# Spectral attention as one unrolled program: transform, attention and taps of three batches side by side, the gate applied in the frequency domain, the next router's logits inside

## The chip, the cores and the metric

One core of one Trainium2 chip. The metric is device time in microseconds (us) of one execution of the whole program, which holds nine blocks of a small hybrid network; the change rewrites one of them and takes in a small one behind it.

## The reference, cut to what matters

The rows are 8,192 tokens (8 batches of 1,024) of 256 channels. Two blocks of the chain are touched: the spectral attention with its residual, and the router logits that the next mixture of experts needs. In each batch, 16 chunks of 64 tokens are transformed:

```python
Xh = jnp.fft.rfft(chunks, axis=2)                  # 33 bins of each chunk and channel
X_low, X_high = Xh[:, :, :4, :], Xh[:, :, 4:, :]
A_low = complex(attention(X_low.real), attention(X_low.imag))   # 16 heads, 4 kv heads, 64 tokens
H_r, H_i = causal_conv(X_high.real), causal_conv(X_high.imag)   # 7 taps, gelu, 256x256 product
g = sigmoid(chunks.mean(axis=2) @ gate_w.T)[:, :, None, :]
A_high = complex(H_r * g, H_i * g) + X_high
Y_hat = concatenate([alpha * A_low + (1 - alpha) * X_low, A_high])
x = x + irfft(Y_hat, n=64)                         # on the layer-normed x; then logits = x @ Wg.T
```

All products are float32.

## The kernel before

`R.X` keeps all rows on the core, as 64 tiles of 128 tokens by 256 channels (8 tiles a batch). Each engine has its own queue, written out by hand; semaphores order them. A `Stage` ends with a barrier of all engines, so nothing of one stage lies beside another. `skewed` writes a loop whose phases run a fixed number of steps behind each other.

`spectral_attention` (L818) is four stages, each over all eight batches, and `raw_logits` (L283) is a fifth:

- **Weights** (`turned_copies`, L782): seven loads, 52 transposes by TensorE, 13 copies by ScalarE (L815).
- **Transform** (L850): VectorE normalizes a tile (L904), TensorE multiplies it by the Fourier matrix (L878), VectorE copies it into the spectrum `XF` (L909). At the end the gates of all chunks are made (L886 to L920) and stored to DRAM.
- **Attention** (L925): an unrolled loop over batches. TensorE makes queries (L955), keys (L961), values (L968), scores (L979, zero-padded queries, 128 rows deep), transposes of the shares (L989), the weighing (L997), the output product (L1004). VectorE makes the softmax (L1081 to L1090) with its exponential on ScalarE (L1042). ScalarE copies the rest.
- **Convolution and inverse** (L1097): sixteen steps of four tiles. VectorE runs 28 tap instructions a step over four accumulators (L1229, L1233), ScalarE the gelu (L1175), TensorE the channel product (L1137), ScalarE its copy (L1184), TensorE the inverse (L1148), the low pass of the normalized tile (L1149) and the inverse of the low bins (L1150). VectorE multiplies by the gate in the time domain (L1213), adds the low term (L1214), normalizes again (L1205) and takes the statistics (L1219). GpSimd adds twice (L1269, L1271).
- **Logits** (`raw_logits`): per tile two transposes (L314), one copy (L335), two products with eight columns (L322). Beside them the rows go out to `sum_dram`.

## Time and profile before

| | |
|---|---|
| median of three runs | 4252.68 us (4248.62 to 4254.37) |
| profiled execution | 4250.82 us, its span 4248.8 us |
| five stages above | from 752.7 to 1374.8 us of the span, 622.1 us |

The profile comes from one execution. PE is the TensorE matmul, PEld its weight load, DVE is VectorE, ACT ScalarE, POOL GpSimd. Two records of a float32 matmul belong together (two passes of two), but a transpose is one record. PEclk is the granted TensorE clock as a share of full speed.

### The profile page before, as it was taken

How to read it: one execution, taken by the hardware profiler on the slowest of the kernel's cores; microseconds unless marked ns; L12 is line 12 of the kernel's file. 1: busy time of each engine (PE TensorE's matmuls, PEld its weight loads, DVE VectorE, ACT ScalarE, POOL GpSimd, SP SyncE). 2: the span in 40 equal slices, each digit the busy share in tenths (PEclk: the TensorE clock that was granted, in tenths of full speed). 3: DMA queues.
4: the chain of work that ended last, by engine and by line, in shares of the span. 5: the costliest groups of instructions: out<-in, count | busy, mean ns of one | idle time of the engine just before them, and what ended most of it. 6: DMA issues, size and time to landing. Idle time of an engine off the chain costs nothing. (4 is left out here: it accounts for less than half of the span.)

```text
span 4248.8 us, 118480 instructions
## 1 busy us (share of the span) xinstructions
PE 3765.7 (89%) x44654; PEld 3235.7 (76%) x44654; DVE 2500.6 (59%) x6817; ACT 2036.2 (48%) x6280; POOL 1392.2 (33%) x1780
## 2 busy tenths in 40 slices
PE   8957998696668499969999999999998799999998
PEld 7857998584437499958888888888885477777775
DVE  5565555536992655544444444444446588888885
ACT  3344554132221555523443443434434488888884
POOL 2225664001331466523333333333333222222214
PEclk9978999797895699989999999999999899999999
DMA  3033444100002444330000000000000000000002
GB/s 109 31 121 97 93 93 110 39 1 26 28 29 94 144 93 93 61 109 3 3 3 3 3 3 3 3 3 3 3 3 9 15 2 2 2 2 2 2 2 88
DMA packets 138456, 162.53 MB, mean 38 GB/s; under 512 B 11984, under 2 KB 128624, under 8 KB 137968
## 3 DMA queue, kind: packets, MB, share of 16 engines
q1 hardware_dynamic: 113392, 122.17, 9.1%
q0 software_dynamic: 24576, 33.57, 4.6%
q8 instruction: 340, 5.57, 0.5%
q14 instruction: 148, 1.21, 0.1%
HBM read 96.85 MB, written 58.85 MB: 37 GB/s over the span
## 5 line engine op out<-in xcount | busy, mean ns | idle before, releaser
L1955 ACT ACTIVATE wa_S<-wa_S,wa_top 128x256 f32<-128x256 f32 x1024 | 511.7, 506 | 139.2 <-DVE wa_top L2019 138.4
L1614 DVE TENSOR_TENSOR so_AB<-so_rows,so_masks 128x1024 f32<-128x1024 f32 x256 | 313.5, 1224 | 243.3 <-PE so_rows L1358 226.1
L2019 DVE CUSTOM_DVE_ANT_0 wa_S<-wa_bank,wa_band 128x256 f32<-128x256 f32 x1024 | 366.9, 419 | 8.4 <-issue 8.3
L1673 POOL TENSOR_TENSOR so_state<-so_compact,so_head 128x384 f32<-128x384 f32 x224 | 185.3, 827 | 335.5 <-PE so_bankC L1425 248.0
L1881 PE MATMUL wa_bank<-ident,wa_S 128*128 128x128 f32 x2048 | 274.4, 275 | 22.2 <-ACT wa_probT L1962 22.2
L1603 DVE SCALAR_TENSOR_TENSOR so_compact<-so_compact,so_bankX 128x96 f32<-128x96 f32 x192 | 48.8, 254 | 414.3 <-PE so_bankX L1461 414.3
L1881 PEld LDWEIGHTS wa_bank<-ident,wa_S 128*128 128x128 f32 x2048 | 230.6, 141 | 67.2 <-ACT wa_S L1955 31.2
L1386 PE MATMUL so_bankJ<-so_xnT,so_w 128*128 128x128 f32 x2048 | 251.5, 276 | 1.2 <-ACT so_QT L1523 0.7
L1386 PEld LDWEIGHTS so_bankJ<-so_xnT,so_w 128*128 128x128 f32 x2048 | 240.4, 193 | 1.9 <-ACT so_QT L1523 1.0
L1549 ACT COPY so_OT<-so_bankC 128x128 f32<-128x128 f32 x256 | 68.1, 266 | 307.7 <-PE so_bankC L1425 307.7
L1668 POOL TENSOR_TENSOR so_Ug<-so_U,so_decay_t 128x128 f32<-128x128 f32 x224 | 102.2, 456 | 325.4 <-ACT so_U L1536 325.4
L1955 ACT ACTIVATION_READ_ACCUMULATOR wa_S<-wa_S,wa_top 128x1 f32 x1024 | 199.3, 195 | 0.0
L713 ACT ACTIVATE m2e_hT<-m_bank,m2e_bias 128x256 fp32r<-128x256 f32 x256 | 126.6, 494 | 150.9 <-PE m_bank L665 145.1
L713 ACT ACTIVATE m4e_hT<-m_bank,m4e_bias 128x256 fp32r<-128x256 f32 x256 | 126.3, 493 | 148.5 <-PE m_bank L665 142.3
L1269 POOL TENSOR_TENSOR spc_high<-spc_high,spc_low 128x256 f32<-128x256 f32 x64 | 49.6, 775 | 447.8 <-DVE spc_low L1214 447.8
L2027 DVE COPY wa_probT<-wa_bank 128x512 f32<-128x512 f32 x256 | 166.9, 687 | 48.3 <-PE wa_bank L1881 47.0
L665 PE MATMUL m_bank<-m2e_exT,m_w_parts 128*128 128x256 f32 x1536 | 190.0, 283 | 0.3 <-ACT m2e_h L713 0.3
L665 PE MATMUL m_bank<-m4e_exT,m_w_parts 128*128 128x256 f32 x1536 | 189.9, 283 | 0.1
L679 PE MATMUL m_bank<-m_w_parts,m4e_hT 128*128 128x256 f32 x1536 | 189.5, 282 | 0.6 <-DVE m4e_pre L760 0.6
L679 PE MATMUL m_bank<-m_w_parts,m2e_hT 128*128 128x256 f32 x1536 | 189.5, 282 | 0.6 <-DVE m2e_pre L760 0.6
L679 PEld LDWEIGHTS m_bank<-m_w_parts,m2e_hT 128*128 128x128 f32 x1536 | 186.3, 188 | 0.8 <-issue 0.8
L679 PEld LDWEIGHTS m_bank<-m_w_parts,m4e_hT 128*128 128x128 f32 x1536 | 186.2, 188 | 0.8 <-issue 0.8
(411 smaller groups left out, 10556.6 us busy)
## 6 DMA issues: line engine op xcount, KB each, us to landing
m_w_raw<-in_L_ffn_W_dram SPq DMA_DIRECT2D x64, 512.0 KB, 3.9
sum_dram<-X SPq DMA_DIRECT2D x16, 1024.0 KB, 4.9
X<-sum_dram SPq DMA_DIRECT2D x16, 1024.0 KB, 7.1
X<-in_L_attn_a_x_dram SPq DMA_DIRECT2D x8, 1024.0 KB, 11.5
xn_dram<-m2r_xn SPq DMA_DIRECT2D x16, 512.0 KB, 3.1
spc_gx<-gate_dram SPq DMA_DIRECT2D x128, 64.0 KB, 2.5
xn_dram<-m4r_xn SPq DMA_DIRECT2D x16, 512.0 KB, 3.1
out_dram<-X SPq DMA_DIRECT2D x8, 1024.0 KB, 4.4
```

The costliest lines, as they stand in the source:

```text
L665: last = nc.tensor.matmul(bank[:, 0:2 * P], w_parts[:, par, a, c, f * P:(f + 1) * P], exT[:, s % 2, b, c], start=(n == 0), stop=(n == len( ...
L679: last = nc.tensor.matmul(by[u][:, 0:HID], hT[:, s % 2, a, f, u * P:(u + 1) * P], w_parts[:, par, b, 2 + f // QF, f % QF * HID:(f % QF + 1 ...
L713: last = nc.scalar.activation(to, bh[f % 4][:, 0:2 * P], ACT.Gelu_apprx_tanh, bias=bias[:, par, f:f + 1])
L1386: last = nc.tensor.matmul(bJ[:, k * P:(k + 1) * P], w[:, n, c, k * P:(k + 1) * P], xnT[:, c * P:(c + 1) * P], start=(c == 0), stop=(c == H ...
L1549: nc.scalar.copy(OT[:, t % (2 * UT)], bC[:, P:2 * P]).then_inc(s_["O_ready"], 1)
L1614: nc.vector.tensor_tensor(AB[:, t % 2].rearrange("p h m t -> p h (m t)"), rows4[:, :, 0:2 * P], masks[:].rearrange("p m t -> p (m t)")[:, ...
L1668: nc.gpsimd.tensor_tensor(Ug[:, t % 2], U[:, t % 2], decay_t[:], ALU.mult).then_inc(s_["Ug_ready"], 1)
L1673: nc.gpsimd.tensor_tensor(state[:, t % UT], compact[:, t % UT, :, None, :].broadcast_to([P, 3, HG, DK]), head[:, None, :, None].broadcast_ ...
L1881: last = nc.tensor.transpose(bT[q % 2][:, (2 * h + k) * P:(2 * h + k + 1) * P], S[:, n % 2, 2 * q + h, k * P:(k + 1) * P], R.ident[:])
L1955: nc.scalar.activation(S[:, n % 2, z], S[:, n % 2, z], ACT.Exp, bias=top[:, n % 2, z:z + 1], scale=-1.0, accum_out=sums[:, i % 2, SET * c ...
L2019: nc.vector.tensor_tensor_reduce(out=S[:, n % 2, z], in0=bS[g][:, eo * SPAN:(eo + 1) * SPAN], in1=band[:], scale=-(D ** -0.5), scalar=3e38 ...
L2027: nc.vector.tensor_copy(probT[:, n % 2, 2 * q:2 * q + 2].rearrange("p h k t -> p (h k t)"), bT[q % 2][:]).then_inc(s_["T_dve"], 1)
```

## The change

`raw_logits` goes, and `spectral_attention` becomes one stage without a loop on the machine: the program is written out for all batches. In iteration `b`, half steps `u = 2b` and `2b+1` (four tiles each) are convolved and finished, batch `b+1` attends, batch `b+2` is read and transformed. `XF` keeps three batches.

- The spectrum drops the two zero sine rows, so that two tiles fill one PSUM bank and are copied in one instruction (`copy_spectrum`, 128x512, four a batch).
- Normalizing is ScalarE's (`normalize`), and ScalarE also adds the normalized row to `R.X` in place (`add_normal`), in place of the low-pass product and the second normalizing on VectorE. The output product subtracts the low bins from the attention result (`XK`, `minus`), and `copy_low` scales it by alpha.
- `close` multiplies the channel product by the gate in the frequency domain while it leaves PSUM. The broadcast gates come in by eight DMAs a batch. Gates are made batch by batch (16 rows by 256).
- One of four accumulators is convolved by TensorE with diagonal matrices (seven products of up to 224 columns), 21 tap instructions a half step stay on VectorE.
- `scores` uses 64-row by 64-column parts of the array. The inverse of the low bins uses 32-row parts, the logits 32-column parts (8 of 32 columns used) followed by one transpose.
- `add_result` adds the inverse to `R.X` straight from PSUM on VectorE, GpSimd no longer adds; it copies the low bins into `XK` (32 small copies a batch).
- A batch of rows goes out to `sum_dram` when it is ready.
- The weights' blocks are turned through six banks, ScalarE and VectorE taking turns, after the transforms of two batches.

```diff
-def raw_logits(nc, R, tag, A):
...
+    CH, LOW, SLOTS, STEPS, G = 64, 4, 3, 2, 4
...
+    ON_PE = (HC - 1, 1)
+    ON_DVE = [(c, r) for c in range(HC) for r in range(2) if (c, r) != ON_PE]
...
+                for b in range(BATCH + 1):
+                    if b < BATCH:
+                        sp.wait_ge(g_ready, b + 1)
+                        sp.dma_start(R.gate_dram[b * CB:(b + 1) * CB, :], g[:]).then_inc(g_stored, 16)
+                        sp.wait_ge(g_stored, 16 * (b + 1))
+                        for s in range(STEPS):
+                            if b >= 1:
+                                sp.wait_ge(H_ready, G * (STEPS * (b - 1) + s + 1))
+                            for r in range(2):
+                                for h in range(2):
+                                    first = b * CB + 2 * G * s + h
+                                    row = r * CH + h * CH // 2
+                                    sp.dma_start(gx[row:row + CH // 2, s],
+                                                 R.gate_dram[None, first:first + 2 * G - 1:2, :].broadcast_to([CH // 2, G, HID])
...
+                                                 ).then_inc(gx_in[s], 16)
+                    if b >= 1:
+                        sp.wait_ge(x_ready, TB * b)
+                        sp.dma_start(R.sum_dram[(b - 1) * SEQ:b * SEQ, :].rearrange("(j p) d -> p j d", p=P),
...
+                def transform(b, n):
+                    m = b * TB // 2 + n
+                    pe.wait_ge(xn_ready, 2 * m + 2)
+                    if m >= 2:
+                        pe.wait_ge(f_ready, m - 1)
+                    if b >= 2 and n < 2:
+                        pe.wait_ge(k_ready, b)
+                        pe.wait_ge(v_ready, b)
+                    for j in range(2):
...
+                def gates(b):
+                    pe.wait_ge(f_ready, (b + 1) * TB // 2)
+                    for c in range(HC):
...
+                def scores(b):
+                    pe.wait_ge(q_ready, 2 * b + 2)
+                    pe.wait_ge(k_ready, b + 1)
+                    if b >= 1:
+                        pe.wait_ge(A_ready, b)
+                    for m in range(PRS):
+                        for r in range(2):
+                            for h in range(2):
+                                rows = slice(h * HD, (h + 1) * HD)
+                                last = nc.tensor.matmul(sbank[m // 4][rows, (m % 4 * 2 + r) * T:(m % 4 * 2 + r + 1) * T],
+                                                        Q[rows, m, r], kT[rows, m // 2, r], start=True, stop=True)
...
+                def convolve(u):
+                    c, r = ON_PE
+                    room = yb[3][:, 0:2 * G * BINS[r]].rearrange("p (n f) -> p n f", n=2 * G)
+                    for tap in range(TAPS - 1, -1, -1):
+                        back = TAPS - 1 - tap
+                        last = nc.tensor.matmul(room[:, :, back:], diag[:, tap], spread(u, c, r, back),
+                                                start=(back == 0), stop=(tap == 0))
+                    last.then_inc(c_done, 1)
...
+                def inverse(u):
+                    b, s = u // STEPS, u % STEPS
+                    if u == 0:
+                        pe.wait_ge(k_loaded, 48)
+                    for k in range(G):
+                        pe.wait_ge(H_ready, G * u + k + 1)
+                        nc.tensor.matmul(yb[k][:, HID:2 * HID], inv_high[:], H[:, k], start=True, stop=False)
+                    pe.wait_ge(A_ready, b + 1)
+                    for k in range(G):
+                        rows = slice(k * 32, (k + 1) * 32)
+                        last = nc.tensor.matmul(yb[k][:, HID:2 * HID], inv_low[rows, s, :], lowA[rows, b % 2, :],
+                                                start=False, stop=True, tile_position=(k * 32, 0))
+                    last.then_inc(Y_done, 1)
...
+                for b in range(-1, BATCH):
+                    u = STEPS * b
+                    attend, read = b + 1 < BATCH, b + 2 < BATCH
+                    if attend:
+                        scores(b + 1)
+                    if b >= 1:
+                        turn_result(u - 1)
+                    if b >= 0 and read:
+                        transform(b + 2, 0)
+                        transform(b + 2, 1)
+                    if b >= 1:
+                        logits(u - 1)
+                    if b >= 0:
+                        convolve(u)
+                    if b >= 1:
+                        turn_logits(u - 1)
+                    if b >= 0:
+                        if read:
+                            transform(b + 2, 2)
+                            transform(b + 2, 3)
+                        channels(u)
+                    if read:
+                        gates(b + 2)
+                    if b >= 0:
+                        inverse(u)
+                    if attend:
+                        turn_probs(b + 1)
+                    if read:
+                        queries(b + 2)
+                    if attend:
+                        weigh(b + 1)
+                    if b >= 0:
+                        turn_result(u)
+                    if read:
+                        keys_values(b + 2)
+                    if b >= 0:
+                        logits(u)
+                        convolve(u + 1)
+                        turn_logits(u)
+                    if attend:
+                        project_out(b + 1)
+                    if b >= 0:
+                        channels(u + 1)
+                        inverse(u + 1)
+                turn_result(LAST - 1)
+                logits(LAST - 1)
+                turn_logits(LAST - 1)
...
+                def normalize(i):
+                    if i >= 4:
+                        act.wait_ge(f_done, i // 2 - 1)
+                    nc.scalar.activation(xn[:, i % 4], R.X[:, i, :], ACT.Identity, scale=R.rstd[:, i:i + 1], bias=R.shift[:, i:i + 1]
+                                         ).then_inc(xn_ready, 1)
+                def add_normal(i):
+                    act.wait_ge(xn_ready, i + 1)
+                    nc.scalar.activation(R.X[:, i, :], R.X[:, i, :], ACT.Identity, scale=R.diff[:, i:i + 1], bias=R.shift[:, i:i + 1]
+                                         ).then_inc(xp_ready, 1)
...
+                for b in range(-1, BATCH):
+                    u = STEPS * b
+                    attend, read = b + 1 < BATCH, b + 2 < BATCH
+                    if b >= 0 and read:
+                        for j in range(4):
+                            normalize((b + 2) * TB + j)
+                    if b >= 1:
+                        copy_result(u - 1)
+                        copy_logits(u - 1)
+                    if b >= 0:
+                        gelu_of_pe(u)
+                    if b >= 1:
+                        place_logits(u - 1)
+                    if b >= 0 and read:
+                        for j in range(4, TB):
+                            normalize((b + 2) * TB + j)
+                    if attend:
+                        exp_probs(b + 1)
+                        exp_gates(b + 1)
+                    if read:
+                        copy_gates(b + 2)
+                    if attend:
+                        copy_probs(b + 1)
+                    if read:
+                        copy_queries(b + 2)
+                    if attend:
+                        if b == -1:
+                            act.wait_ge(alpha_ready, 1)
+                        copy_values(b + 1)
+                    if b >= 0:
+                        copy_result(u)
+                    if read:
+                        copy_keys_values(b + 2)
+                    if b >= 0:
+                        copy_logits(u)
+                        gelu_of_pe(u + 1)
+                        gelus(u + 1)
+                        place_logits(u)
+                    if attend:
+                        copy_low(b + 1)
+                    if b >= 0 and read:
+                        for j in range(TB):
+                            add_normal((b + 2) * TB + j)
+                    if attend:
+                        gelus(u + 2)
...
+                def convolve(u):
+                    if u >= 2:
+                        dve.wait_ge(gel_dve, NDVE * (u - 1))
+                    done = NDVE * (TAPS - 1) * u
+                    for tap in range(TAPS - 1, -1, -1):
                         back = TAPS - 1 - tap
+                        for n, (c, r) in enumerate(ON_DVE):
+                            to = acc[:, u % 2, n, :, back:BINS[r]]
+                            if back == 0:
+                                ins = nc.vector.tensor_scalar(to, spread(u, c, r, back), dw[:, c, r, tap:tap + 1], None, ALU.mult)
+                            else:
+                                dve.wait_ge(taps, done + NDVE * (back - 1) + n + 1)
+                                ins = nc.vector.scalar_tensor_tensor(out=to, in0=spread(u, c, r, back), scalar=dw[:, c, r, tap:tap + 1],
+                                                                     in1=to, op0=ALU.mult, op1=ALU.add)
...
+                def close(u):
+                    s = u % STEPS
+                    dve.wait_ge(gx_in[s], 16 * 4 * (u // STEPS + 1))
+                    if u >= 1:
+                        dve.wait_ge(Y_done, u)
+                    for k in range(G):
+                        dve.wait_ge(H_done, G * u + k + 1)
+                        nc.vector.tensor_tensor(H[:, k], yb[k][:, 0:HID], gx[:, s, k], ALU.mult).then_inc(H_ready, 1)
...
+                def add_result(u):
+                    dve.wait_ge(Y_done, u + 1)
+                    dve.wait_ge(xp_ready, TB * (u // STEPS + 1))
+                    for k in range(G):
+                        row = R.X[:, tile_of(u, k), :]
+                        nc.vector.tensor_tensor(row, row, yb[k][:, HID:2 * HID], ALU.add).then_inc(x_ready, 1)
...
+                for b in range(-1, BATCH):
+                    u = STEPS * b
+                    attend, read = b + 1 < BATCH, b + 2 < BATCH
+                    if attend:
+                        shift_scores(b + 1)
+                    if b >= 0 and read:
+                        copy_spectrum(b + 2, 0)
+                        copy_spectrum(b + 2, 1)
+                    if attend:
+                        share_scores(b + 1)
+                        close_gates(b + 1)
+                    if b >= 0:
+                        if read:
+                            copy_spectrum(b + 2, 2)
+                            copy_spectrum(b + 2, 3)
+                        close(u)
+                        if read:
+                            low_part(b + 2)
+                        add_result(u)
+                        convolve(u + 1)
+                    if attend:
+                        convolve(u + 2)
+                    if b >= 0:
+                        close(u + 1)
+                        add_result(u + 1)
...
+                for b in range(BATCH):
+                    pool.wait_ge(f_ready, (b + 1) * TB // 2)
+                    if b >= 2:
+                        pool.wait_ge(A_done, b - 1)
+                    for c in range(HC):
+                                    first = b % SLOTS * CB + 2 * (G * t + k)
+                                    ins = nc.gpsimd.tensor_copy(XK[:, b % 2, c, k, r, t].rearrange("p (h f) -> p h f", f=LOW)[:, :, r:],
+                                                                XF[:, c, first:first + 2, r * CH // 2 + r:r * CH // 2 + LOW])
+                    ins.then_inc(XK_ready, 1)
...
         spectral_attention(nc, R, A, C)
-        raw_logits(nc, R, "l4", A)
         top_k_experts(nc, R, "m4", A, C, 1)
```

Functions of the new program that are not shown do what their names say: `turn_probs`, `queries`, `weigh`, `keys_values`, `project_out` as before for one batch; `channels` 16 products with 256 columns a half step; `exp_probs` and `exp_gates` the exponentials, `copy_...` a copy out of PSUM by ScalarE, `shift_scores` and `share_scores` the two halves of the softmax, `close_gates` an add and a reciprocal of 16x256.

## Rows read from the trace of the kernel before

**Rows 1.** The page: the span, and TensorE's busy time in it.

```profile
span 4248.8 us, 118480 instructions
PE 3765.7 (89%) x44654; PEld 3235.7 (76%) x44654; DVE 2500.6 (59%) x6817; ACT 2036.2 (48%) x6280; POOL 1392.2 (33%) x1780
```

**Rows 2.** Busy by stage: stretch, length, PE, PEld, DVE, ACT, POOL, clock, DMA.

```profile
752.70:776.80 24.10, 9.45 (x52) 7.23 (x52) 0.00 (x0) 7.39 (x13) 0.00 (x0) 0.64 0.42 142
776.80:830.60 53.80, 43.40 (x260) 35.64 (x260) 47.53 (x141) 3.41 (x5) 0.00 (x0) 0.91 0.02 4
830.60:995.80 165.20, 143.02 (x1376) 131.85 (x1376) 55.57 (x89) 56.02 (x98) 0.00 (x0) 0.91 0.01 1
995.80:1295.80 300.00, 189.03 (x896) 117.29 (x896) 283.31 (x769) 73.32 (x193) 100.80 (x128) 0.86 0.10 30
1295.80:1374.80 79.00, 75.89 (x386) 75.77 (x386) 13.59 (x32) 12.66 (x34) 0.00 (x0) 0.50 0.33 107
```

**Rows 3.** Timeline of TensorE, attention: start, duration, line, count, idle before.

```profile
842.77 3.76 PE L979 MATMUL sp_bank<-spa_kT,spa_Qd 128*128 128x64 f32 x32 [0.55 <-ACT spa_v L1036]
846.36 3.79 PE L955 MATMUL sp_bank<-spa_XL,sp_qwT 128*128 128x128 f32 x32
849.99 1.95 PE L961 MATMUL sp_bank<-spa_XL,spa_kwd 128*128 128x128 f32 x16
851.77 1.03 PE L968 MATMUL sp_bank<-sp_vwT,spa_XL 128*128 128x256 f32 x4
...
967.41 1.09 PE L989 MATMUL sp_bank<-ident,spa_probs 128*128 128x128 f32 x8 [0.70 <-DVE spa_probs L1090]
969.23 1.91 PE L997 MATMUL sp_bank<-spa_pT,spa_v 64*64 64x64 f32 x64 [0.73 <-ACT spa_pT L1047]
```

**Rows 4.** Timeline of TensorE, convolution: one tile of four, from product to inverse.

```profile
1136.22 0.42 PE L1137 MATMUL sp_bank<-sp_pwT_r,spc_gel 128*58 128x256 f32 x1
...
1136.93 0.38 PE L1137 MATMUL sp_bank<-sp_pwT_i,spc_gel 128*58 128x256 f32 x1
1137.24 0.70 PE L1148 MATMUL sp_bank<-spc_H,spc_inv_high 128*128 128x256 f32 x2
1137.78 0.59 PE L1149 MATMUL sp_bank<-spc_xn,spc_low_pass 128*128 128x256 f32 x2
1138.21 0.59 PE L1150 MATMUL sp_bank<-sp_lowA,spc_inv_low 128*128 x2
```

**Rows 5.** Groups of instructions in the attention stage: busy, mean ns, idle before.

```profile
L1081 DVE SCALAR_TENSOR_TENSOR spa_probs<-sp_bank,spa_mask 128x512 f32<-128x512 f32 x16 | 11.0, 685 | 3.4 <-PE sp_bank L979 3.1
L1085 DVE TENSOR_REDUCE spa_tops<-spa_probs 128x16 f32<-128x1024 f32 x8 | 9.7, 1215 | 0.3
L1042 ACT ACTIVATE spa_probs<-spa_probs 128x1024 f32<-128x1024 f32 x8 | 8.5, 1060 | 0.0
L1054 ACT COPY sp_lowA<-sp_bank 128x256 f32<-128x256 f32 x8 | 3.0, 372 | 37.7 <-PE sp_bank L1004 37.7
L920 DVE RECIPROCAL spf_g<-spf_g 128x256 f32<-128x256 f32 x1 | 1.8, 1752 | 0.0
```

**Rows 6.** Timeline of VectorE in the convolution stage.

```profile
996.71 4.30 DVE L1233 SCALAR_TENSOR_TENSOR spc_acc<-sp_XF,sp_dw,spc_acc 128x224 f32<-128x224 f32 x12
...
1126.84 3.02 DVE L1233 SCALAR_TENSOR_TENSOR spc_acc<-sp_XF,sp_dw,spc_acc 128x208 f32<-128x208 f32 x6
...
1131.34 0.41 DVE L1213 TENSOR_TENSOR spc_high<-sp_bank,spc_gx 128x256 f32<-128x256 f32 x1
1131.67 0.48 DVE L1214 SCALAR_TENSOR_TENSOR spc_low<-sp_bank,sp_alpha,spc_xn 128x256 f32<-128x256 f32 x1
1132.06 1.39 DVE L1219 BATCH_NORM_STATS2 raw<-X  x4
```

**Rows 7.** Timeline of ScalarE in the router stage behind the change.

```profile
1382.34 1.28 ACT L478 ACT_TABLE_LOAD   x1
1383.63 0.63 ACT L478 ACTIVATE m4r_Lx<-m4r_Lx 128x512 f32<-128x512 f32 x1
...
1392.19 2.56 ACT L470 ACTIVATE m4r_xn<-X,shift,rstd 128x256 f32<-128x256 f32 x5 [1.90 <-DMA xn_dram<-m4r_xn]
```

**Rows 8.** Busy by stretch at the attention's end, columns as in rows 2.

```profile
976.00:984.00 8.00, 3.11 (x23) 2.23 (x22) 2.70 (x3) 2.50 (x4) 0.00 (x0) 0.87 0.01 2
984.00:992.00 8.00, 7.32 (x71) 6.24 (x70) 0.00 (x0) 1.17 (x2) 0.00 (x0) 0.50 0.00 0
```

839 lines of the change are left out of this document (398 added, 441 removed).

## The prediction

> **What bounds the kernel now.** The page comes first: TensorE is busy for 89% of the span [rows 1], but that is an average over nine blocks, and five stages alone are rewritten. So the second view is the busy time by stage [rows 2]. It shows five stretches, 622.1 us together (24.1 + 53.8 + 165.2 + 300.0 + 79.0), with a different limit in each. In the transform VectorE is busy for 47.5 of 53.8. In attention it is TensorE, 143.0 of 165.2. In the convolution it is VectorE, 283.3 of 300.0, while TensorE works 189.0. In the logits TensorE is busy for 75.9 of 79.0, at a granted clock of 0.50, the lower of its two levels (1.2 GHz; full is 2.4 GHz). The sum is what matters for a change that lays these stages beside each other: TensorE 460.8, VectorE 400.0, ScalarE 152.8, GpSimd 100.8. Neither engine fills the 622.1. The third view is the timelines, for prices of single operations, since group means mix two clocks.
>
> **TensorE's work for one batch in the new order.** Prices at full clock, as differences between starts, so that a stream is priced and not the tail of its last record. Queries: 849.99 - 846.36 = 3.63 us for 16 matmuls of 128 columns, 0.23 each [rows 3]. Keys: 851.77 - 849.99 = 1.78. A matmul of 256 columns is two records: 1138.21 - 1137.78 = 0.43 [rows 4].
>
> - read (transform, 16 of 128 columns 3.7, gates 0.9, queries 3.7, keys 1.8, values 0.9): 11.0
> - scores: the trace has them 128 rows deep, 3.6 us (846.36 - 842.77). The new ones are 32 matmuls of 64x64 by 64 columns, as many and of the shape of the weighing, 1.91 [rows 3]. Bounds 1.9 and 3.6; I take 1.9, because row count, shape and columns all agree
> - transposes of shares 1.0, weighing 1.9 [rows 3]
> - output product: 8 of 256 columns 3.4, and 2 of 128 for the subtraction 0.5: 3.9
> - taps on TensorE: 7 products of about 200 columns, 0.43 x 200/256 = 0.33 each, twice: 4.7
> - channel products: from the first to the next stage's first record 1137.24 - 1136.22 = 1.02 a tile [rows 4]; 8 records, in pairs side by side, make 4 x 0.21 = 0.86 of it, the rest belongs to the switch below: 8 x 0.86 = 6.9
> - inverse: 8 of 256 columns 3.4; the low bins, 8 on 32-row parts, lie between all four side by side (2 x 0.43 = 0.9) and one after another (3.4); I take 1.7, as the 64-row parts in the weighing overlap about twofold (64 records of 64 columns in 1.91, against 64 x 0.21 x 64/256 = 3.4 if they did not)
> - transposes of the result 16 x 0.13 = 2.1; logits between 0.9 (four side by side) and 3.4, 1.8 taken; their transposes 0.3
>
> Sum: 11.0 + 1.9 + 1.0 + 1.9 + 3.9 + 4.7 + 6.9 + 5.1 + 2.1 + 1.8 + 0.3 = 40.6 us. Where the array changes between whole and parts, the next matmul starts 0.31 behind the last one (1137.24 - 1136.93) where 0.21 is the pitch: 0.1 for a switch [rows 4]. An iteration has some 16: 1.6. So 42.2.
> The Trainium skill, TensorEngine Tiling (Array Packing), Key Properties, speaks against this change here: a change of tiling mode drains TensorE. The trace agrees in kind, with that 0.1 us; the page gives no price, and if the whole tail of a record (0.38 - 0.21 = 0.17) were paid at each switch the sum would grow by another 1.1 us a batch.
>
> **VectorE.** Two score passes 1.4 and four passes of 1024 columns, 1.22 each, 4.9 [rows 5], a small reciprocal 0.3; gates 0.3 + 1.75 (the reciprocal of 256 columns takes 1752 ns whatever the rows); spectrum 4 x 0.69 (priced as the 128x512 pass of L1081) = 2.8; low bins 0.7; `close` 8 x 0.33 and the additions 8 x 0.33, both from 1131.67 - 1131.34, statistics 8 x 0.35 [rows 6]: 8.1 together; taps 42 x 0.36 = 15.1. Sum 35.4. The tap's price is 4.30/12 = 0.36 where GpSimd is idle; where GpSimd adds beside it, it is 3.02/6 = 0.50 [rows 6]. GpSimd's adding goes, so I take 0.36 and keep 0.50 as the other bound.
>
> **ScalarE.** 16 normalizings and additions at 2.56/5 = 0.51 [rows 7] = 8.2; three score and gate operations 1.5; copies of 512 columns 5 x 0.59 and of 256 about 15 x 0.37 [rows 5] = 8.5; gelus 8 x 0.4, logits 0.9; two table loads 2.6, because exponential and gelu alternate. About 25 us of work, not a bound by its sum, but its place in the chain counts.
> A load takes 1.28 us, and the next operation starts 0.01 behind it and the load 0.02 behind what was before [rows 7]. The Trainium skill, ScalarE: Activation LUTs, section What ACT_TABLE_LOAD costs, puts a drain of about 1.38 us beside each load. The trace does not show it (0.02 us); by the page the chain below would be some 1.4 us longer in each batch, about 10 us in all.
>
> **One iteration, followed.** t = 0 is the end of `inverse(u-1)`; queues are served in their written order. TensorE: scores to 1.9, transposes to 3.0, transforms 0 and 1 to 4.8, logits to 5.7, taps to 8.1. Transform 2 needs normalized tiles 4 and 5. ScalarE has them at 9.9, as it first turns out the last batch's result (to 4.2), the logits and the gelu of TensorE's accumulator (to 8.6). So 1.7 us idle. Transforms end at 11.9, channel products at 15.3. `gates` now needs the last spectrum copy. VectorE's chain to it: additions and statistics to 3.0, scores' first half to 7.0, spectrum copies to 8.4, then a wait for the exponential. ScalarE comes to it behind the normalizings: 10.9, load 12.2, exponential 13.3. Second half of the softmax to 16.1, gates 18.1, spectrum copies 19.4. TensorE waits 15.3 to 19.5: 4.2 us, the largest idle time. From there: gates, inverse (`close` ends 20.9) to 22.9, transposes 24.0, queries 27.7, weighing 29.6, result 30.6, keys and values 33.3, logits, taps, output product to 40.6, channel products 44.0, inverse 45.8. VectorE meanwhile: additions 25.9, two times 21 taps to 41.1, `close` behind the channel products. ScalarE is never last in this half.
> So 45.8 us, and with 1.6 for the switches 47.4. Clock: in attention TensorE is busy for 87% and the clock is 0.91 [rows 2]. At that stage's end there are 8 us in which TensorE worked only 3.1, and the 8 behind them had 0.50 [rows 8]; the gap of 4.2 would do the same on a smaller scale. At 0.91, 42.2 of work becomes 46.4; 4.2 more, of which the part in front of the gap (15 us of 42) is swallowed by it: 2.7. **x = 50 us an iteration.** The reads (batches 0 and 1) stand ahead, so iteration 6 has no read part (41 us by the same walk) and iteration 7 no attention (37).
>
> **Ahead of the loop.** From 752.7: scales and the first exponential with its table 5; ScalarE's 32 normalizings and additions 16.4, with the transforms and the weights' arrival beside them; seven weight copies 4; gates, queries, keys, values of batch 0 8; iteration -1 (scores 2, softmax 8, transposes, queries, weighing, keys 9, output product 4) 23. Some 58 with handoffs. The last rows' way out and the stage's end add 2.5.
> New stages: 58 + 6 x 50 + 41 + 37 + 2.5 = 438.5 in place of 622.1: 183.6 saved. 4250.8 - 183.6 = 4067.2 in terms of the profiled execution (its span 4248.8 and 2.0 around it). That execution lies 1.9 below the median of 4252.7, so the median becomes **4069 us**. Nothing behind the stage changes: `top_k_experts` takes `R.L` and `R.X` as before. The unrolled code costs nothing, as the attention stage was unrolled too, with 1376 matmul records in 165 us and TensorE 143 of them busy [rows 2].
>
> **Rivals.** Each is priced as 58 + 7.56x + 2.5 (7.56 = 6 + 78/50).
>
> - *The gap closes* (the exponential comes earlier, switches are free): x = 44, TensorE's work and little else. 229 saved: 4024. For it: 143.0 of 165.2 busy in attention without much tuning of waits. Against it: `gates` stands behind VectorE's whole softmax in every batch.
> - *VectorE becomes the bound*: GpSimd's 32 copies a batch slow the taps to 0.50, 42 x 0.14 = 5.9 more, in the chain addition, taps, taps, `close`; or each of a dozen handoffs costs 0.5 more than I gave. x = 56: 138 saved: 4114. For it: rows 6. Against it: 32 copies of 8 columns are short beside 35 us.
> - *The lower clock holds* (the other side): TensorE stays at 1.2 GHz as in the logits stage, where it was busy all along and still had 0.50 [rows 2]. Work 84.4 a batch, x = 84.4: 58 + 638 + 2.5 = 698.5, 76 more than 622: 4329. It decides from x = 74, that is with 60% of the work at the lower clock. Against it: the logits' eight-column products are gone, and attention, busy likewise, had 0.91.
> - *It overlaps less than written*: a wait I did not see makes the batches run one after another. VectorE's 35.4 and half of TensorE's 42.2 in turn, x = 60 to 70: 4145 to 4220.
>
> **Chances.** Forecast 0.62 (its own range 4045 to 4095), closed gap 0.13, VectorE or handoffs 0.15, less overlap 0.05, lower clock 0.05. About 0.2% (8.5 us) is what a measurement of this kernel can tell from no change. Faster 0.94, within it 0.01, slower 0.05. The range takes the two neighbours: 4015 to 4125.
>
> **What would show it.** Right: a stage of about 438 us, eight repeats of about 50 us, TensorE busy for 85% or more in them with its longest wait ahead of the 16-row gate product, VectorE at about 35 us a batch, taps at 0.36, clock near 0.9. `close` and `add_result` wait for TensorE, not for the gates' DMAs. Wrong: taps at 0.5, a clock near 0.5 with TensorE busy, table loads with idle time behind them, 32-row parts one after another (1.7 more a batch), or an idle time of ScalarE ahead of `copy_gates` that holds the queries' copies back.

## The result, and the profile after

The changed kernel takes 4062.6 us (median of 4 runs, 4060.7 to 4066.8), the kernel before 4250.7 us beside it: a ratio of 0.956, interval 0.955 to 0.957. The forecast was 4069, in a range of 4015 to 4125 (the forecast's own part of it 4045 to 4095). The profiled execution took 4066.8 us, span 4065.0, and is the slowest of the four; the forecast put it at 4067.2. The page, as in [rows 1]:

```profile
span 4065.0 us, 117344 instructions
PE 3666.4 (90%) x45082; PEld 3162.5 (78%) x45082; DVE 2378.9 (59%) x6470; ACT 2074.4 (51%) x6364; POOL 1334.1 (33%) x1919
```

The one new stage runs from SyncE's first load at 754.33 us to the next stage's first load at 1183.19: 428.9 us in place of 622.1, so 193.2 are saved there, and 183.8 in the span. Busy time by stretch, columns as in [rows 2]; the cuts lie where TensorE comes to the scores of each iteration (the second one, at 817.6, is 1.7 us early: the first score matmul there starts at 819.27, so that the part ahead takes 64.9 us and the first iteration 47.0):

```profile
754.30:817.60 63.30, 44.37 (x381) 40.70 (x382) 30.31 (x66) 31.76 (x62) 15.27 (x75) 0.82 0.25 77
817.60:866.00 48.40, 41.73 (x400) 34.09 (x398) 30.76 (x75) 24.27 (x53) 4.14 (x32) 0.96 0.06 17
866.00:911.80 45.80, 40.89 (x426) 33.63 (x418) 33.39 (x83) 22.57 (x53) 4.14 (x32) 1.00 0.15 47
911.80:959.20 47.40, 42.49 (x426) 34.41 (x418) 33.37 (x83) 22.51 (x53) 4.14 (x32) 0.96 0.15 46
...
1101.50:1140.80 39.30, 32.74 (x338) 25.51 (x330) 30.11 (x75) 12.36 (x31) 0.00 (x0) 0.91 0.17 51
1140.80:1171.20 30.40, 23.36 (x182) 16.57 (x174) 15.70 (x45) 5.16 (x17) 0.00 (x0) 0.94 0.16 51
1171.20:1183.20 12.00, 2.64 (x32) 1.32 (x25) 2.73 (x8) 1.82 (x6) 0.00 (x0) 0.73 0.26 88
```

First the part ahead of the loop, then full iterations (the three left out are like the one from 911.8 us: 47.4 or 47.5), then iterations 6 and 7 and the end. TensorE is busy for 86 to 90% of a full iteration, VectorE for 33.4 us, ScalarE for 22.5. In the iteration at full clock 40.9 us of TensorE's work and 4.9 of waiting make 45.8. Its timeline in the iteration from 912 us, with all its idle time (starts, durations, counts, idle before):

```profile
912.02 2.08 PE L954 MATMUL sp_bank<-sp_kT,sp_late 64*64 64x64 f32 x64
914.03 1.09 PE L1035 MATMUL sp_bank<-ident,X 128*128 128x128 f32 x8
914.96 1.95 PE L893 MATMUL sp_bank<-sp_dft,sp_xn 128*128 128x128 f32 x16
916.84 0.64 PE L1042 MATMUL sp_bank<-sp_late,sp_wgT 128*32 128x128 f32 x16
917.41 2.64 PE L1000 MATMUL sp_bank<-sp_XF,sp_diag 128*128 128x224 f32 x14
...
921.56 2.14 PE L893 MATMUL sp_bank<-sp_dft,sp_xn 128*128 128x128 f32 x16 [1.40 <-ACT sp_xn L1115]
...
930.82 1.70 PE L916 MATMUL sp_bank<-sp_gwT,sp_XF 128*16 128x256 f32 x4 [3.51 <-DVE sp_XF L1301]
932.45 2.98 PE L1023 MATMUL sp_bank<-sp_late,sp_inv_high 128*128 128x256 f32 x8
935.36 0.71 PE L1027 MATMUL sp_bank<-sp_lowA,sp_inv_low 32*128 32x256 f32 x8
```

There are two waits, at the two places that the walk had: 1.40 us before transform 2, for the normalized tiles, and 3.51 us before the 16-row gate product, for the last spectrum copy. VectorE and then ScalarE show what is in front of that copy:

```profile
918.63 1.28 DVE L1301 COPY sp_XF<-sp_bank 128x512 f32<-128x512 f32 x2
924.89 1.22 DVE L1331 TENSOR_REDUCE sp_sums<-sp_late 128x16 f32<-128x1024 f32 x1 [4.97 <-ACT sp_late L1152]
926.14 0.25 DVE L1332 RECIPROCAL sp_sums<-sp_sums 128x16 f32<-128x16 f32 x1
926.43 1.23 DVE L1333 TENSOR_TENSOR sp_late<-sp_late,sp_sums 128x1024 f32<-128x1024 f32 x1
927.58 0.27 DVE L1337 TENSOR_SCALAR sp_g<-sp_g 16x256 f32<-16x256 f32 x1
927.88 1.74 DVE L1339 RECIPROCAL sp_g<-sp_g 16x256 f32<-16x256 f32 x1
929.55 1.21 DVE L1301 COPY sp_XF<-sp_bank 128x512 f32<-128x512 f32 x2
...
939.52 6.18 DVE L1353 SCALAR_TENSOR_TENSOR sp_acc<-sp_XF,sp_dw,sp_acc 128x224 f32<-128x224 f32 x18
```

```profile
920.09 0.36 ACT L1185 ACTIVATE sp_gel<-sp_bank 128x224 f32<-128x224 f32 x1 [2.27 <-PE sp_bank L1000]
...
920.41 2.08 ACT L1115 ACTIVATE sp_xn<-X,shift,rstd 128x256 f32<-128x256 f32 x4
922.50 1.28 ACT L1152 ACT_TABLE_LOAD   x1
923.80 1.06 ACT L1152 ACTIVATE sp_late<-sp_late 128x1024 f32<-128x1024 f32 x1
```

ScalarE waits 2.27 us for TensorE's taps before a gelu, only then normalizes tiles 4 to 7 (TensorE waits for two of them), loads the table and raises to the exponential. VectorE has waited 4.97 us for that. It ends the softmax, closes the gates (2.0 us) and only then copies the spectrum that TensorE waits for. Behind the gap the clock is down (busy by stretch):

```profile
911.80:927.80 16.00, 14.11 (x175) 11.63 (x167) 10.50 (x18) 7.88 (x17) 0.00 (x0) 1.00 0.27 90
927.80:931.80 4.00, 0.98 (x3) 0.40 (x4) 3.97 (x8) 0.00 (x0) 0.98 (x8) 0.91 0.02 4
931.80:935.80 4.00, 4.00 (x18) 2.48 (x16) 0.79 (x5) 0.36 (x1) 3.16 (x25) 0.66 0.48 131
935.80:959.20 23.40, 23.40 (x239) 19.90 (x231) 18.11 (x54) 14.26 (x35) 0.00 (x0) 1.00 0.04 8
```

0.66 lies between the two levels, so both were granted within these 4 us; ahead of the gap and from 935.8 us on the clock is 1.00. Five of the six full iterations have such a stretch; those behind the first take 47.4 us, and the one without it (from 866 us) took 45.8: the fall costs 1.6.

### The profile page after: what moved, and what is told of

It is laid out like the page before. It is cut to its first block and busy times, and to the rows that moved or that the text cites. A ratio compares the mean times of both kernels' runs of the same rounds, so it can differ in the third digit from the quotient of the medians.

```text
span 4065.0 us, 117344 instructions
## 1 busy us (share of the span) xinstructions
PE 3666.4 (90%) x45082; PEld 3162.5 (78%) x45082; DVE 2378.9 (59%) x6470; ACT 2074.4 (51%) x6364; POOL 1334.1 (33%) x1919
## 5 line engine op out<-in xcount | busy, mean ns | idle before, releaser
L596 PEld LDWEIGHTS m_bank<-m2e_exT,m_w_parts 128*128 128x128 f32 x1536 | 185.5, 191 | 0.0
```

Of the source, the lines that this page charges most:

```text
L596: last = nc.tensor.matmul(bank[:, 0:2 * P], w_parts[:, par, a, c, f * P:(f + 1) * P], exT[:, s % 2, b, c], start=(n == 0), stop=(n == len( ...
```

## The experiments

Each is held against the changed kernel (4062.6 us, stage 428.9) if nothing else is said. They were measured at other times than that kernel; the kernel before, measured beside each group, had medians of 4248.8 to 4250.7 us, so differences of a few us between medians say little by themselves, and the lengths in the profiles are read with them. "Stage" goes from the first load of the stage to that of the experts behind it, in the profile.

**The gates later on VectorE** (`gates_late`). In VectorE's loop:

```diff
                         share_scores(b + 1)
-                        close_gates(b + 1)
...
                     if attend:
                         convolve(u + 2)
+                        close_gates(b + 1)
```

> Only the place of one small VectorE operation changes: the gates of the next batch are closed behind the last taps, and not in the middle of the softmax. Nothing is left out. Theory (VectorE's chain to the 16-row gate product sets the first half of each iteration, and the clock's fall behind that gap is part of its price): VectorE has 1.75 us less (a reciprocal of 256 columns) ahead of the last spectrum copy, so TensorE's wait of 3.51 us before the gate product shrinks to about 1.5 to 2, the lower clock behind it goes (1.6 us), a full iteration falls from 47.4 us to about 44 to 45.7, and the whole kernel by 13 to 22 us. Rival (VectorE's second half is itself at its limit, so that the work only moves): the gates then delay the closing of the channel products, the wait reappears before the inverse, and the kernel moves by 0 to -5 us.

Measured: 4041.8 us (4039.9 to 4048.4; ratio to before 0.951, 0.950 to 0.953), 20.8 less. The stage is 405.4 us and every full iteration behind the first 43.9. Two of them by stretch, and TensorE's waits in five of them (total, times, longest):

```profile
861.70:905.60 43.90, 40.90 (x424) 33.64 (x420) 33.37 (x83) 22.56 (x53) 4.09 (x32) 1.00 0.17 52
905.60:949.50 43.90, 40.90 (x424) 33.64 (x420) 33.38 (x83) 22.56 (x53) 4.09 (x32) 1.00 0.17 50
```

```profile
PE sp_bank L916 <- DVE sp_XF L1301: 8.0, 5, 1.6
PE sp_bank L893 <- ACT sp_xn L1115: 7.0, 5, 1.4
```

The theory holds: the wait falls from 3.5 to 1.6 and the clock is 1.00 behind both waits. VectorE does the same 33.4 us of work as before, and nothing waits for what was moved: 1.9 of waiting and 1.6 of clock are gone in each iteration.

**Normalizings earlier on ScalarE** (`normals_early`).

```diff
+                    if b >= 0 and read:
+                        for j in range(4, TB):
+                            normalize((b + 2) * TB + j)
                     if b >= 0:
                         gelu_of_pe(u)
                     if b >= 1:
                         place_logits(u - 1)
-                    if b >= 0 and read:
-                        for j in range(4, TB):
-                            normalize((b + 2) * TB + j)
```

> Only ScalarE's order changes: the four normalizings of tiles 4 to 7 come before the gelu of TensorE's accumulator instead of behind it. Nothing is left out. Theory (ScalarE's queue holds transform 2, and the exponential behind it): TensorE's 1.40 us before transform 2 go, the table load and the exponential begin about 2.1 us earlier because ScalarE no longer waits for TensorE's taps, VectorE's 5 us wait for them shrinks to about 3, and the gap before the gate product shrinks with it: a full iteration 47.4 -> 43.7 to 45.3 us, the kernel -13 to -21 us. Rival (the gelu's own load moves the wait to the channel products or to the exponential: it needs its table, and the exponential cannot begin before it in this order): the gap before transform 2 goes, but the exponential stays where it is, and the kernel moves by at most -3 us.

Measured: 4053.3 us (4051.1 to 4056.1), 9.3 less, outside both. Two iterations by stretch, then waits in five:

```profile
864.35:909.81 45.46, 42.16 (x423) 34.43 (x419) 33.32 (x83) 22.55 (x53) 4.20 (x32) 0.96 0.15 47
909.81:956.53 46.72, 43.43 (x422) 34.90 (x418) 33.32 (x83) 22.54 (x53) 4.20 (x32) 0.93 0.15 47
```

```profile
PE sp_bank L916 <- DVE sp_XF L1301: 16.5, 5, 3.3
...
DVE sp_sums L1331 <- ACT sp_late L1152: 15.1, 5, 3.0
```

The first wait is gone and the exponential comes 2 us earlier (VectorE's wait 5.0 -> 3.0), as the theory has it. But TensorE too reaches the gate product 1.8 us earlier in the iteration, so the gap there shrinks only from 3.5 to 3.3, and the clock still falls behind it, in every second iteration for longer (0.93). That is where the expected size went wrong: I had let both waits shrink at once, and counted the clock as regained.

**Both moves** (`both`).

> Both moves together, VectorE's gates behind the last taps and ScalarE's normalizings before the gelu. Nothing is left out. Theory: no wait of TensorE over 1 us is left in an iteration, its clock stays at 1.00 in most of it, and an iteration is TensorE's 40.9 us at full clock and about 0.8 of handoffs: 41.7 us, six times 5.7 less, the kernel about -34 us, -25 to -38. Rival (VectorE's 33.4 us of work and its waits for the products take over as the bound): iteration 45 us, the kernel -10 to -18 us, with TensorE waiting for the closing of the channel products.

Measured: 4031.1 us (4027.2 to 4034.7; ratio 0.948, 0.947 to 0.950), 31.5 less; stage 397.1, and each full iteration behind the first 41.9 us:

```profile
900.10:942.00 41.90, 40.51 (x424) 33.53 (x420) 33.39 (x83) 22.53 (x53) 4.09 (x32) 1.00 0.18 53
```

The size comes out as expected: 40.5 us of TensorE and one wait of 1.4. But a wait over 1 us is left, against the expectation, and in the old place: the gate product still waits for VectorE's last spectrum copy. For the rest of the iteration TensorE is busy; that VectorE takes over as the bound, as the rival had it, is not seen.

**The gap filled with useless work** (`filler`).

```diff
                 def gates(b):
+                    if b >= 2:
+                        pe.wait_ge(shifted, b)
+                        for _ in range(15):
+                            nc.tensor.matmul(sbank[0][:, 0:P], R.ident[:], R.ident[:], start=True, stop=True)
                     pe.wait_ge(f_ready, (b + 1) * TB // 2)
```

> The changed kernel, with 15 useless matmuls of 128 columns (identity by identity, about 0.22 us each at full clock, 3.3 us) put on TensorE ahead of its wait for the last spectrum copy before the 16-row gate product, in the six full iterations; the output does not depend on them. They fill most of the 3.51 us in which TensorE stood idle and add work, and shorten no chain. Theory (the idle gap itself lowers the granted clock behind it, 0.66 in 931.8 to 935.8 us, and that costs 1.6 us an iteration): the clock is 1.00 behind the filler, full iterations fall from 47.4 to 45.8 us, the kernel is 6 to 10 us faster although it does 20 us more of TensorE work. Rival (the clock falls for another reason, as the work itself, or the useless matmuls delay what waits): iteration 47.4 us or more, the kernel 0 to +6 us.

Measured: 4057.9 us (4057.2 to 4066.1), 4.7 less by the medians; the profile has 421.0 in the stage, 7.9 less, and 45.8 us in each full iteration behind the first. The filler in TensorE's timeline, and the iteration:

```profile
924.12 3.62 PE L917 MATMUL sp_bank<-ident 128*128 128x128 f32 x30
927.71 1.05 PE L920 MATMUL sp_bank<-sp_gwT,sp_XF 128*16 128x256 f32 x4
```

```profile
908.90:954.69 45.79, 44.39 (x452) 37.05 (x449) 33.38 (x83) 22.53 (x53) 4.14 (x32) 1.00 0.16 48
```

3.6 us more of TensorE's work in each iteration, and the iteration is 1.6 us shorter. The gate product starts 18.8 us into the iteration, as in the changed kernel (930.82 - 912.02), so no chain became shorter; what is gone is the idle time and, with it, the lower clock behind it. So the fall needs the idle time, and 1.6 us is its price. The median's 4.7 is less than the 6 to 10 expected and lies within the spread of the runs (9 us); the reading rests on the profile.

The idle time doesn't always bring the fall. The iteration from 866 us had the same wait of 3.51 and kept 1.00. In the profile of `more_sems2` (below), whose instructions in the loop are the same, it is the next one that keeps it, with the same two waits of 1.4 and 3.5:

```profile
911.00:956.78 45.78, 40.87 (x422) 33.61 (x418) 33.37 (x83) 22.53 (x53) 4.11 (x32) 1.00 0.16 48
```

So it isn't the work of one iteration that decides it; what does stays open.

**All taps on VectorE** (`taps_vector`). `ON_PE`, its `convolve` on TensorE and `gelu_of_pe` go; `ON_DVE` has all four accumulators.

> All four accumulators of the short convolution are built on VectorE (56 taps a batch and not 42), none on TensorE; the result is the same function. TensorE has 14 products less a batch (4.7 to 5.3 us), VectorE 14 taps more (5 us at 0.36) and the gelu of TensorE's accumulator becomes part of the other ones. Theory (a chain through all engines sets the iteration, TensorE only the second half of it): VectorE's second half grows to 38 us of work in all and gives back what TensorE saves; iteration 46.5 us give or take 1.5, the kernel -15 to +8 us. Rival A (TensorE's amount of work is the bound): iteration 47.4 - 5 = 42.5 us, the kernel about -35 us. Rival B (VectorE is already the bound behind the gap): iteration 52 us, the kernel +35 us.

Measured: 4062.2 us (4060.7 to 4064.3), 0.4 less; the full iterations take 44.3, four times 47.1 to 47.5, and 46.5 us, with TensorE at 39.3 and VectorE at 37.4 in the four. Waits in five iterations:

```profile
PE sp_bank L915 <- DVE sp_XF L1270: 16.0, 5, 3.5
PE sp_bank L1008 <- DVE sp_late L1333: 12.3, 5, 2.5
```

The chain theory holds. The gap before the gate product stays, and TensorE now also waits in the second half, for the closing of the products (L1333): at 37.4 us VectorE's second half has become late too. With 14 products less TensorE is busy only 3.2 us less (39.3 for 42.5), as the granted clock is 0.93 for 0.96. TensorE's amount of work is not what bounds the changed kernel, and convolving one accumulator there is by itself worth nothing in the total.

**The batches not side by side** (`serial`). The new order on TensorE, which takes the place of the mixed one (behind it come the transforms, gates, queries, keys and values of batch b+2; ScalarE and VectorE likewise):

```diff
+                    if attend:
+                        scores(b + 1)
+                        turn_probs(b + 1)
+                        weigh(b + 1)
+                        project_out(b + 1)
+                    if b >= 0:
+                        for w in (u, u + 1):
+                            convolve(w)
+                            channels(w)
+                            inverse(w)
+                            turn_result(w)
+                            logits(w)
+                            turn_logits(w)
+                    if read:
...
```

> The changed kernel's own instructions, in another order: on every engine's queue the attention of batch b+1 comes first, then both steps of the convolution, products, inverse and logits of batch b, then transform, gates, queries, keys and values of batch b+2, and not the three mixed. Nothing is left out. Theory (laying three batches side by side is what takes the place of the idle time, about half of the saving): an iteration is 62 to 72 us with TensorE busy for about 42, the kernel +100 to +175 us against the changed one, 4165 to 4240 us, so near that of before. Rival (the saving comes from less work and from TensorE's higher clock, and the engines' queues run ahead of each other by themselves): iteration under 54 us, the kernel +0 to +50 us.

Measured: 4185.8 us (4183.7 to 4191.1), 123.2 more than the changed kernel and 1.5% less than before (0.985, 0.984 to 0.987). The stage takes 548.3 us. An iteration, and three of the waits in five of them:

```profile
951.30:1016.50 65.20, 48.78 (x419) 38.58 (x418) 34.27 (x83) 23.40 (x52) 4.12 (x32) 0.87 0.11 33
```

```profile
DVE sp_late L1319 <- PE sp_bank L1012: 52.9, 40, 5.9
DVE sp_late L1278 <- PE sp_bank L954: 41.5, 10, 8.1
...
PE sp_bank L962 <- DVE sp_late L1288: 36.4, 5, 7.3
```

This divides the 193.2 us of the stage: 73.8 (622.1 - 548.3) come from what is computed and where, 119.4 (548.3 - 428.9) from laying batches side by side. That holds for this one order; another unmixed order, with other waits, could share it out differently, and the 73.8 were not divided further. TensorE's work alone shows the clock once more: 48.8 us at 0.87 for what took 40.9 at 1.00.

**The logits outside again** (`logits_outside`). `turn_result`, `logits`, `turn_logits` and ScalarE's three copies leave the stage; `raw_logits` stands behind it without its stores.

> Only the gate logits leave the unrolled stage: the transposes of the result, the logit products, their transposes and ScalarE's copies around them go, and the separate logits stage of the kernel before stands behind it again, without its stores of the rows (they stay in the unrolled stage). Theory (they cost inside what TensorE needs for them and a part of their handoffs, 2.9 to 4.5 us a batch, and outside a stage of 77 to 79 us at the lower clock): the unrolled stage 24 to 36 us shorter, the kernel +43 to +55 us against the changed one. Rival (inside they lie in TensorE's waiting time and cost nothing): the kernel +70 to +79 us.

Measured: 4122.3 us (4121.0 to 4124.6), 59.7 more: between the two, nearer the theory. The unrolled stage is 407.2 us, 21.7 less (24 to 36 were expected), its full iterations 42.4 to 45.3. The stage behind it, by stretch:

```profile
1162.00:1240.00 78.00, 75.89 (x386) 75.77 (x386) 13.59 (x32) 12.70 (x34) 0.00 (x0) 0.50 0.00 1
```

It is still the lower clock, 0.50, that makes this stage dear, without the stores too. Inside, the same logits cost 2.7 us a batch; I had put them at 2.9 to 4.5. So this part alone is worth 57 of the 193 us (486.2 for both stages against 428.9). It is no third addend to the 73.8 and 119.4; it overlaps with them.

**A best version** (`best`): both moves, and three small ones. ScalarE's additions for batch 0 come behind the weight copies, those for batch 1 behind `copy_keys_values` in iteration -1; VectorE's last taps come before `close(u)`; the last batch's rows leave in two stores.

```diff
-                for i in range(2 * TB):
-                    add_normal(i)
...
+                for i in range(TB):
+                    add_normal(i)
                 for b in range(-1, BATCH):
...
+                        if not attend:
+                            convolve(u + 1)
                         close(u)
```

> Both moves (gates behind the last taps, normalizings before the gelu) and three small ones outside the full iterations: ScalarE adds the normals of the first two batches behind the weight copies instead of ahead of them, in the last iteration VectorE's last taps come before the closing of the products, and the last batch's rows are stored in two halves. Nothing is left out. Theory (TensorE's 4.65 us before the weights' transposes and its 4.53 us before the last channel products go, and the store ends 1 to 2 us earlier): 8 to 13 us less than with both moves alone, 4018 to 4024 us. Rival (the additions only hold back the copies of queries and values in the first iteration, and the stage's end waits for something else): 0 to 5 us less.

Measured: 4016.7 us (4011.9 to 4017.6; ratio 0.945, 0.943 to 0.946), 14.4 less than with both moves alone, a little more than the 8 to 13 expected. In the profile 7.0 of it are ahead of the loop (64.9 -> 57.9) and 6.3 from iteration 6's start to the stage's end (81.2 -> 74.9).

**28 semaphores more** (`more_sems2`).

```diff
+        for n in range(28):
+            sem(f"unused{n}")
```

> The changed kernel with 28 semaphores more in the stage, which nothing signals or waits for; the stage's end clears them on GpSimd with its other 76. One profile. Theory (from ScalarE's last copy, which ends at 1175.46, to the next stage's first DMA at 1183.19 it takes 7.73 us in the changed kernel, of which 76 clearings are about 5, 0.065 each): that stretch is 1.8 us longer, 9.5 us. Rival (the stretch is the store of the last rows and the barriers, and clearing costs nothing): 7.7 us.

The last copy of ScalarE starts at 1171.20 and takes 0.18, and SyncE's first load of the next stage is at 1180.93:

```profile
1171.20 0.18 ACT L1207 COPY L<-sp_bank 128x32 f32<-128x32 f32 x1 [0.42 <-PE sp_bank L1050]
```

```profile
1180.93 0.32 SPq L350 DMA_DIRECT2D m4r_wg_rows<-in_L_ffn_Wg_dram  x1
```

9.55 us where the changed kernel has 7.73: 1.82 for 28 clearings, 0.065 each. By that price the 76 of the stage are 4.9 us of its end. The trace of the changed kernel has the clearings themselves: SyncE's wait for the last store of rows ends at 1177.4, and GpSimd's 76 clearings start at 1177.73 to 1182.84, 0.064 apart with one pause of 0.3. So the 7.73 are about 1.9 for the store, 5.1 for the clearing and 0.7 for the barriers. (One execution: 4065.5 us; by its time alone nothing could be told.)

**Clearing on four engines** (`clear_split2`): the best version, and in `Stage.__exit__` each of GpSimd, VectorE, ScalarE and SyncE clears every fourth semaphore.

```diff
-                    for s in self.sems:
-                        pool.sem_clear(s)
+                    for s in self.sems[0::4]:
+                        pool.sem_clear(s)
...
+                    for s in self.sems[1::4]:
+                        dve.sem_clear(s)
```

> The best version so far, where each stage's end clears its semaphores on four engines, a quarter each, and not all on GpSimd. Nothing is left out. Theory (clearing is serial on one engine, 0.065 us each): the stretch from ScalarE's last copy of the spectral stage to the next stage's first DMA falls from 6.2 us by 3.7 to about 2.5, the other stages' ends give another 1 to 4 us together, the kernel -4 to -8 us against that version, 4009 to 4013 us. Rival (the four engines clear through one port, or the store of the last rows ends no earlier): 0 to -1.5 us.

Measured: 4010.3 us (4005.7 to 4015.1; ratio 0.944, 0.942 to 0.945), 6.4 less than the best version; the runs of the two overlap (4011.9 to 4017.6 there), so that by the times alone the gain is near what the noise allows. The stretch at the stage's end falls from 6.22 to 3.05 us, 3.2 where 3.7 were expected. This is the fastest version by its median, 1.3% below the changed kernel.

**The kernel before once more** (`before_again2`).

> The kernel before, unchanged, for a second profile of its experts' stage behind the rewritten one. It was 478.0 us there and 481.1 to 484.0 in the profiles of the changed kernel and its variants, with TensorE waiting up to 1.6 us for a gather of rows. Theory (that belongs to the new stage): 477 to 479 us again. Rival (it differs from run to run): anything between 478 and 484.

4251.3 us. The experts' stage took 476.8 us there (1370.63 to 1847.46), after 478.0 in the first profile. In the changed kernel it was 484.0, and in nine variants 481.1 to 485.3 (the expectation's range left out 485.3), in `clear_split2` 478.6. So some 3 to 8 us there seem to come with the new stage in front of it; in `logits_outside`, where the old logits stage stands between, it is 481.6 too. But other unchanged stretches moved by as much between the two profiles of the kernel before: what stands behind the experts' stage took 2396.0 and 2401.8 us.

## Why the prediction was right

The places of both waits in the iteration and the order of the engines were right, and so was the mechanism behind each of them. The total was nearer than the terms, and that is luck: in the profile the stage is 9.6 us shorter than forecast and the rest of the kernel 9.4 longer. In terms of the profiled execution, forecast and measured (up to iteration 6 from first score matmul to first score matmul):

| term | forecast | measured |
|---|---|---|
| ahead of the loop | 58 | 64.9 |
| six full iterations | 6 x 50 = 300 | 282.5 (45.8 to 47.5) |
| iteration 6 | 41 | 39.1 |
| iteration 7 | 37 | 30.4 |
| end of the stage | 2.5 | 12.0 |
| stage | 438.5 | 428.9 |
| outside the stage | 0 | +9.4 (1.6 ahead of it, 6.0 in the experts' stage, 1.8 behind) |

- **A full iteration**, 50: 47.4. Of the 2.7 (50.1 - 47.4) the work is 0.6, the waits 1.0 and the clock 1.1. The walk held 39.9 us of work (45.8 less 5.9 of waiting) and not the 40.6 of the sum.
- **TensorE's work**, 40.6 and 1.6 for switches: 40.9 to 42.5 busy, 40.9 at full clock. The taps there take 2.48 us a time (919.89 - 917.41, the next operation's start, with a switch ahead of them) and not 2.35, the logits 0.57 and not 0.9, the low bins 0.65 and not 0.85. All four 32-row parts start within 0.02 us of each other, two groups of 0.3 us, so they lie side by side, near the lower of the two bounds (1.3 us a batch, for 0.9 and 3.4). Switches cost more than the 0.1 read in rows 4. The iteration from 866 us has 16: the first matmul behind one starts 0.09 to 0.10 late (0.309 behind the last where the pitch is 0.216), and the next one again 0.02 to 0.10 late (0.320 where the pitch is 0.216), 2.5 us together for 1.6. The Trainium skill, TensorEngine Tiling (Array Packing), Key Properties, says that a change of tiling mode drains TensorE; the trace agrees in kind, and its 2.5 us are near the 2.7 that the whole tail of a record at each of them would make. The single prices were lower by more than that.
- **VectorE's 35.4**: 33.4. Taps 6.18/18 = 0.34, not 0.36, and GpSimd's 32 copies (4.1 us) lie beside the inverse and not beside the taps, so the price of 0.50 never came up. The reciprocal of 256 columns takes 1.74 us on 16 rows, as assumed. In `taps_vector`, at 37.4 us, TensorE begins to wait for VectorE in the second half (2.5 us).
- **The chain to the gate product**, 4.2 us of waiting: 3.5. The 1.7 before transform 2: 1.4. `gates_late` and `normals_early` show both causes, each by moving what was named.
- **The clock**, 2.7: 1.6 in four of five iterations from 866 us on, none in one. The mechanism was right (a gap, then a lower clock), the size was too large: the forecast charged all the 27 us of work behind the gap at 0.91, and the trace has 1.00 again from 935.8 us, some 4 us behind the gap's end. `filler` shows that the fall goes when the gap is filled. Why one iteration, with the same gap of 3.51, kept 1.00 was not settled.
- **Ahead of the loop**, 58: 64.9. TensorE waits 4.65 us for the first weight copy, as ScalarE has 16 additions of 0.5 us in its queue in front. I had counted them and let the weights' transposes run beside them, and overlooked that half the copies of those transposes stand behind the additions. `best` moves them and has 57.9, where the same cuts give 64.9 in `both`.
- **Iteration 7 and the end**, 37 and 2.5: 30.4 and 12.0, together 42.4 for 39.5. Of the 12.0, 4.3 are TensorE's and ScalarE's last transposes and logits (1171.2 to 1175.5), which no term of the forecast names, and 7.7 are the way to the next stage. In proportion the 2.5 was the term most wrong: it priced the rows' way out (about 1.9) and not the clearing, about 5 us for 76 semaphores (`more_sems2`). The trace of the kernel before had the price: at the end of the stage ahead of the change, 28 clearings start at 750.39 to 752.37. Why iteration 7 is 6.6 shorter than forecast was not taken apart.
- **Nothing changes behind the stage**: by the profiles 3 to 8 us longer in the experts' stage. In the changed kernel TensorE waits there for gathers of rows after the first one too (five times, 1.62 us at most), and in neither profile of the kernel before. The difference lies behind the first gathered rows: from their first transpose to the stage's end it takes 409.8 and 410.3 us before, 416.0 after. Whether the gathers are issued or land later, and why, stays open; no run here took it apart.
- **Table loads**: 0.02 us from the load's end to the exponential's start (922.50 + 1.28 and 923.80), and nothing idle in front of it. The Trainium skill, ScalarE: Activation LUTs, What ACT_TABLE_LOAD costs, has a drain of about 1.38 us beside each load; the trace of this kernel shows none, and the measurement decides.
- **The rivals.** None came about in the changed kernel. The closed gap (44 us an iteration) is what `gates_late` makes of it (43.9), and both moves go below (41.9). VectorE is not the bound (33.4 us, taps at 0.34). The overlap is there: without it, in `serial`, an iteration takes 65.2 us, inside that rival's 60 to 70. The lower clock did not hold: 0.96 in the full iterations against 0.50 in the logits' own stage. One sign named as wrong is half there: ScalarE stands idle for 7.39 us ahead of `copy_gates`; but the copies of the queries behind it wait for TensorE's products, so nothing is held back.

## What to carry to other kernels

When several stages are laid beside each other, follow one iteration by hand through each engine's queue: the sum of work (40.9 us here) said little about which reorder would pay, the walk named both waits, and moving one 2-us operation off that chain gave 21 us. A gap in TensorE's work can be charged twice, once as idle time and once by the clock behind it (3.5 and 1.6 us here, in five of six iterations; gaps of 1.6 and 1.4 us cost no clock), so look first at the largest gap and not at the largest group. And price a stage's ends: first copies queued behind work that nobody waits for yet, and the clearing of semaphores on one engine, were 4.65 and about 5 us.

## What was not expected of the hardware

- 3.6 us of useless matmuls in a gap made an iteration 1.6 us shorter, as the clock stayed at 1.00.
- Clearing a semaphore takes 0.065 us on one engine, and engines do it beside each other: on four, the stretch from the last copy to the next stage fell by 3.2 us.
- Full iterations repeat when no wait lowers the clock: five of 43.87 or 43.88 us between their starts with the gates later, five of 41.91 with both moves.
- Behind a change between the whole array and parts of it not one matmul but two start late, by 0.09 to 0.10 and 0.02 to 0.10 us.
